# A fused transformer block on one core: constants, first stack and norm chain of the start-up arranged anew

## The chip, the cores and the metric

The kernel runs on one core of a Trainium2 chip. Its engines are TensorE (PE, with PEld for weight loads), VectorE (DVE), ScalarE (ACT), GpSimd (POOL) and SyncE (SP); DMAs are issued from SP and ACT. Each engine takes its instructions in the order of its own program and waits at semaphores. The metric is the time of one execution on the device, in microseconds, as the median of the runs. Lower is better.

## The reference

For eight batches of 512 tokens with 256 features: a modulated layer norm, causal attention with 16 heads of width 16, a gated residual; then a second modulated norm and a feed-forward block that itself starts with a norm (gain and bias), attention with 32 heads of width 8 without a mask, a residual, and an expert layer in which each half of a batch goes through one expert. All of it is f32.

```python
mod = (_silu(L0_c) @ L0_wmod).reshape(L0_c.shape[0], 6, 1, -1)
sa, ca, ga, sb, cb, gb = (mod[:, 0], mod[:, 1], ...)
h = _layernorm(x, axis=-1) * (1 + ca) + sa
x = x + ga * _L0_attn_ref(h, ...)          # causal, 16 heads of 16
h = _layernorm(x, axis=-1) * (1 + cb) + sb
x = x + gb * _L0_ffn_ref(h, ...)
...
xn = (x - mu) / jnp.sqrt(var + 1e-05) * ln_g + ln_b
att = jnp.einsum('bqhd,bkhd->bhqk', q, k) / np.float32(np.sqrt(hd))   # 32 heads of 8
o = jnp.einsum('bhqk,bkhd->bqhd', p, v).reshape(B, S, D) @ wo + x
h = jax.nn.gelu(jnp.einsum('metd,edf->metf', xe, w1) + b1[None, :, None, :], approximate=False)
y = jnp.einsum('metf,efd->metd', h, w2) + b2[None, :, None, :]
```

## The kernel before

**Plan.** One list of items, written out by hand in `sections()`, sets the order of the work; every engine walks the same list (`walk`) and takes from each item its own part. The sections are "start", "scale", "first", "second", "before" (together the start-up), "loop" (run six times) and "after". An item such as `("scores", 1, 0, 4, 2)` names kind, batch (0 or 1 ahead), attention (0 is the causal one, 1 the second), step and head of the step. `attention(main, lead, beside, ...)` lays out steps: for each position the scores of a step of `main`, the maxima of a step of `lead` (seven or eight steps ahead), the values of the step before, and from `beside` whatever is placed at a slot, four slots to a step. A step is a group of four heads and one 128-row tile; four steps make a group; the causal attention has 16 steps per batch, the second 32.

**Stacks.** Q and k are split into bf16 parts of which the matmuls need several (`qk`: ScalarE writes the top part at L937, VectorE the rest at L1399, GpSimd splits it at L794 and L796, SP stores the parts to DRAM at L711). `stacks` loads them as q_stack and k_stack, 8 heads to a unit (`load_stack`, L640). Three buffers of each are used in turn. The stacks also hold rows of constants: blank slices of q_parts (zeros) and eight rows of ones under each half of k_stack; they meet the rows of the maxima, which `max_rows` writes into q_stack (L730). Before, SP makes them by 12 DMAs from a tile of zeros and 6 from a tile of ones (L748 to L755), right after the first loads, behind two memsets of GpSimd (L781, L782).

**The start.** x of batch 0 is loaded and its norm begun ("start"); an inverse root is made by a first guess on VectorE (L1327 to L1331) and 13 Newton steps on GpSimd (L881 to L889). x of batch 1 is loaded into the same tile once batch 0 is normed. "first" has q and k of batch 0, with batch 1's statistics between the pieces; "second" has v and the first stack (q from SP, k from ACT). ACT issues all weight loads at its start, those of the feed-forward block too (L911), and VectorE rearranges two of them (L1510) before it enters "before".

**The second part of "before"** is the attention of batches 0 and 1, 32 steps in one row (`main`). It is laid out in two pieces, the first 24 steps and the last 8 (`half`). Beside steps 18 to 24 stand the first batch's output projection (L1241), its norm 1 with modulation (L1337, L1341) and the statistics of norm 2; between the pieces stand norm 2 (L1372), its turn to features, q and k of attention 2 (L1117) and their stack; the second piece has beside it v, and ahead of it the maxima of the first eight steps of attention 2 (L1413), two steps at a time in the first two positions.

## Time and profile before

| | |
|---|---|
| median of 3 runs | 1758.55 us (1752.73 to 1762.74) |
| profiled execution | 1755.25 us, span 1753.5 us |
| busy PE, DVE, ACT, POOL | 1495.6 (85%), 1153.1 (66%), 1007.8 (57%), 531.6 (30%) |
| chain that ended last | PE 64%, DVE 16%, ACT 8%, issue 5%, DMA 3% |
| granted TensorE clock, mean | 0.97 |

In the page's 40 slices, PE's digit is low in the first five (5, 6, 8, 6, 6), with PEclk below 9 in three of them; the DMA digit is 9 in the first. A timeline row gives start and length of an instruction or of several of one kind in a row, and in brackets how long its engine was idle before it and what ended that. A chain row gives one piece of the chain that ended last. A "q" behind an engine's name is its queue, that is, the issuing of DMAs.

### The profile page before, as it was taken

What the parts mean: (1) busy time and instruction counts of PE and PEld (TensorE: products, weight loads), DVE (VectorE), ACT (ScalarE), POOL (GpSimd) and SP (SyncE); (2) the same over time, 40 slices, a digit from 0 to 9 for tenths busy, and PEclk for the clock granted to TensorE, in tenths of its full rate; (3) what the DMA queues carried; (4) which work ended last, traced back from release to release, by engine and by line L of the source; (5) the groups of instructions that cost most, each with busy time, mean ns of one, the idle gap of its engine ahead of it and who ended that gap; (6) DMA issues with size and microseconds to landing.
All of it is one profiled execution on the core that took longest, in us unless ns stands there. A gap on an engine that the chain in (4) does not pass through costs nothing.

```text
span 1753.5 us, 30245 instructions
## 1 busy us (share of the span) xinstructions
PE 1495.6 (85%) x10001; PEld 662.1 (38%) x10001; DVE 1153.1 (66%) x2961; ACT 1007.8 (57%) x2096; POOL 531.6 (30%) x1245
## 2 busy tenths in 40 slices
PE   5686689988899889989899889998899887879767
PEld 4232323344333543345233443335333442314315
DVE  4566389755986469764996469763897458775430
ACT  1153357754677456754677456765577546666571
POOL 4233235222433134232343225231352224300100
PEclk9698799999999999999999999999999999999999
DMA  9550434423345233422443242342343232212201
GB/s 260 129 122 31 115 94 127 99 83 97 104 106 134 79 97 115 97 85 76 130 125 98 75 138 89 82 126 76 110 137 89 82 82 77 74 46 73 86 1 60
DMA packets 137542, 171.26 MB, mean 98 GB/s; under 512 B 17000, under 2 KB 103080, under 8 KB 137392
## 3 DMA queue, kind: packets, MB, share of 16 engines
q1 hardware_dynamic: 131568, 164.96, 33.8%
q10 hardware_dynamic: 5824, 4.37, 1.0%
q8 instruction: 86, 1.41, 0.3%
q14 instruction: 64, 0.52, 0.1%
HBM read 110.67 MB, written 56.66 MB: 95 GB/s over the span
## 4 chain that ended last, share of the span: by engine, by line
PE 64%; DVE 16%; ACT 8%; issue 5%; DMA 3%; POOL 2%; SPq 1%; ACTq 0%; POOLq 0%; DVEq 0%
PE bank_out L1198 16%; PE bank_scores L1179 10%; DVE neg_max L1413 8%; PE bank_max L1150 7%; PE bank_side L1285 7%; PE bank_side L1117 5%; ACT probs L976 5%; PE bank_side L1127 4%; PE bank_side L1269 3%; PE bank_scores L1269 3%; PE bank_side L1207 2%; PE bank_side L1241 2%; PE bank_side L1250 2%; DVE normed L1372 2%; DMA k_stack<-k_parts 1%
## 5 line engine op out<-in xcount | busy, mean ns | idle before, releaser
L976 ACT ACTIVATE probs<-bank_scores 128x512 f32<-128x512 f32 (+3 forms) x1536 | 753.2, 544 | 411.5 <-PE bank_scores L1179 394.2
L1413 DVE TENSOR_REDUCE neg_max<-bank_max 128x1 f32<-128x512 f32 x1024 | 653.1, 682 | 185.4 <-PE bank_max L1150 180.7
L1179 PE MATMUL bank_scores<-q_stack,k_stack 64*128 64x512 bf16 (+3 forms) x2048 | 318.0, 347 | 92.9 <-ACT probs L976 78.6
L1198 PE MATMUL bank_out<-probs,v_tile 128*9 128x512 f32 (+4 forms) x3072 | 368.7, 552 | 16.1 <-ACT out_raw L990 12.4
L1150 PE MATMUL bank_max<-k_stack,q_stack 64*128 64x512 bf16 (+3 forms) x2048 | 316.7, 345 | 73.6 <-DVE neg_max L1413 36.9
L1410 DVE CUSTOM_DVE_ANT_0 bank_max<-bank_max,causal 128x384 f32<-128x384 f32 (+3 forms) x512 | 241.8, 514 | 101.9 <-PE bank_max L1150 99.0
L1179 PEld LDWEIGHTS bank_scores<-q_stack,k_stack 64*128 64x128 bf16 x2048 | 84.9, 93 | 368.6 <-issue 348.0
L830 POOL TENSOR_SCALAR_AFFINE_SELECT probs<-probs 128x512 f32<-128x512 f32 x128 | 81.0, 633 | 351.3 <-ACT probs L976 351.2
L1150 PEld LDWEIGHTS bank_max<-k_stack,q_stack 64*128 64x128 bf16 x2048 | 105.6, 95 | 157.5 <-issue 108.6
L812 POOL CAST max_parts<-max_row 16x128 bf16<-16x128 f32 x96 | 28.4, 296 | 361.7 <-DVE max_row L1424 361.7
L1285 PE MATMUL bank_side<-w_out,hidden_T 128*128 128x256 f32 x512 | 118.8, 385 | 4.8 <-issue 2.7
L1285 PEld LDWEIGHTS bank_side<-w_out,hidden_T 128*128 128x128 f32 x512 | 94.6, 190 | 35.0 <-DVE max_row L1424 11.1
L1198 PEld LDWEIGHTS bank_out<-probs,v_tile 128*9 128x9 f32 (+1 forms) x3072 | 47.5, 91 | 133.7 <-issue 78.6
L1459 DVE TENSOR_TENSOR y_out<-bank_side,gb_bc 128x256 f32<-128x256 f32 x32 | 13.6, 425 | 122.9 <-PE bank_side L1285 122.9
L1117 PE MATMUL bank_side<-act_T,wk 128*128 128x256 f32 x236 | 67.4, 409 | 10.8 <-DVE rest L1399 6.5
L794 POOL CAST partsq<-rest 128x256 bf16<-128x256 f32 x64 | 25.4, 397 | 167.6 <-DVE rest L1399 167.6
L1117 PE MATMUL bank_side<-act_T,wq 128*128 128x256 f32 x232 | 69.0, 422 | 8.0 <-DVE act_T L1385 4.3
L1127 PE MATMUL bank_side<-wv,act_T 128*128 128x256 f32 x244 | 70.6, 413 | 4.3 <-ACT act_T L961 2.0
L1410 DVE DVE_READ_ACCUMULATOR2_ANT neg_max<- 128x1 f32 x512 | 72.3, 141 | 0.0
L1207 PEld LDWEIGHTS bank_side<-ident,out_raw 128*128 128x128 f32 x384 | 40.5, 141 | 74.8 <-issue 73.1
L1207 PE MATMUL bank_side<-ident,out_raw 128*128 128x128 f32 x384 | 62.6, 286 | 6.9 <-DVE rest L1399 3.5
L1269 PE MATMUL bank_side<-expert_xT,w_in 128*128 128x256 f32 x256 | 63.5, 391 | 1.5 <-DVE expert_xT L1452 0.9
(141 smaller groups left out, 1529.7 us busy)
## 6 DMA issues: line engine op xcount, KB each, us to landing
q_stack<-q_parts SPq DMA_DIRECT2D x128, 256.0 KB, 4.3
k_stack<-k_parts SPq DMA_DIRECT2D x122, 192.0 KB, 6.1
w_in<-in_L_ffn_w_dram SPq DMA_DIRECT2D x16, 1024.0 KB, 5.5
w_out<-in_L_ffn_w_dram SPq DMA_DIRECT2D x16, 1024.0 KB, 8.5
q_parts<-partsq SPq DMA_DIRECT2D x32, 384.0 KB, 2.6
k_parts<-partsk SPq DMA_DIRECT2D x32, 384.0 KB, 2.6
q_parts<-partsq SPq DMA_DIRECT2D x32, 256.0 KB, 2.9
k_parts<-partsk SPq DMA_DIRECT2D x32, 256.0 KB, 3.0
```

What stands on the lines that cost most here:

```text
L830: pool.affine_select(out=tile, in_=tile, compare_op=ALU.is_ge, fill=0.0, base=0, pattern=[[0, GROUP], [1, P]], channel_multiplier=-1).then ...
L976: nc.scalar.activation(probs[s % 2][:, head_at(k), q0:S], region[bank][:, q0:S], ACT.Exp, scale=float(WIDTH[a]) ** -0.5).then_inc(drained[ ...
L1117: ins = pe.matmul(region[bank][:, 0:S // 2], w_qkv[a][t][:, cc, oc * P:(oc + 1) * P], act_T[:, cc, cols], start=(cc == 0), stop=(cc == C - 1))
L1127: ins = pe.matmul(region[bank][:, 0:D], act_T[:, cc, t * P:(t + 1) * P], w_qkv[a][2][:, cc, :], start=(cc == 0), stop=(cc == C - 1))
L1150: ins = pe.matmul(region[to][:, 0:keys], q_stack[buf][rows, at, qt * P:(qt + 1) * P], k_stack[buf][rows, at, 0:keys], start=(i == 0), stop ...
L1179: ins = pe.matmul(region[to][:, q0:S], k_stack[buf][rows, at, kt * P:(kt + 1) * P], q_stack[buf][rows, at, q0:S], start=(i == 0), stop=last)
L1198: ins = pe.matmul(outb[32 * k:32 * k + WIDTH[a] + 1, q0:S], v_tile[a][:, kt, g * GROUP + k, :], probs[s % 2][:, k, q0:S], start=(kt == 0), ...
L1207: ins = pe.transpose(side[:, t * P:(t + 1) * P], out_raw[:, g % 2, t * P:(t + 1) * P], ident[:, :])
L1269: ins = pe.matmul(region[bank][:, k * EXP_TOK:(k + 1) * EXP_TOK], w_in[:, cc, ft * P:(ft + 1) * P], expert_xT[:, cc, j * EXP_TOK:(j + 1) * ...
L1285: ins = pe.matmul(region[bank][:, 0:D], hidden_T[:, ft, k * P:(k + 1) * P], w_out[:, ft, :], start=(ft == 0), stop=(ft == FT - 1))
L1410: v.tensor_tensor_reduce(region[bank][:, 0:keys], region[bank][:, 0:keys], causal[:, S - keys:S], 1.0, -3e38, ALU.add, ALU.max, dst).then_ ...
L1413: v.tensor_reduce(dst, region[bank], AX_X, ALU.max).then_inc(drained[bank], 1)
```

## The change

- The ones are no longer stored by DMAs: the whole of each k_stack is set to 1.0 on chip, two of the three by VectorE as its first work, the third (buffer 0) by GpSimd after its part of "first"; the loads write the product rows over it. GpSimd sets only a quarter of the zeros, and of the blank slices only those of batch 0's first attention are stored at the start (2 DMAs); the other 6 go out behind the first stack.
- The first stack is loaded by `load_first_stack` in two halves of four heads, 8 DMAs of half the size each for q and k; the first maxima wait for the first half (`half_loaded`), the fifth step for all.
- ACT issues the feed-forward weights after that stack; their rearranging on VectorE becomes the item `ffn_weights`, placed at slot 12 beside the first maxima. The expert bias has a semaphore of its own (`b1_in`).
- The Newton steps of norms 1 and 2 of batch 0 are taken by VectorE.
- The row of 32 steps is cut at step 20 instead of 24, norm 1 stands in one piece ahead of the eleventh maxima of batch 1, and the eight steps of attention 2's maxima stand one by one beside the last eight steps. Some loads (`stacks`, `load_mod`, `load_gate`) move by a slot or two.

```diff
@@ sections()
-    before = [("stacks", 0, 1)]
+    before = []
     beside = {}
+    place(beside, 4, [("stacks", 0, 1)])
+    place(beside, 12, [("ffn_weights", 0)])
...
-    place(beside, 25, [("stacks", 1, 0)])
+    place(beside, 22, [("stacks", 1, 0)])
...
-    place(beside, 79, norm_1[1:NEWTON_PIECE + 1], 0)
+    place(beside, 79, norm_1[1:], 0)
     place(beside, 82, [("load_residual", 1), ("load_gate", 0)])
-    place(beside, 83, norm_1[NEWTON_PIECE + 1:] + norm_2[:NEWTON_PIECE + 1], 0)
-    place(beside, 91, [("load_mod", 1)])
-    half = 3 * len(main) // 4
+    place(beside, 80, norm_2[:NEWTON_PIECE + 1], 0)
+    place(beside, 82, [("load_mod", 1)])
+    half = 20
     left = []
-    before += attention(main[:half], ahead[FIRST_LEAD:], beside, early, left, rows_after=(1, ROWS_AFTER),
+    before += attention(main[:half], ahead[FIRST_LEAD:half + FIRST_LEAD + 1], beside, early, left, rows_after=(1, ROWS_AFTER),
...
-    lead = [(), (), tuple(first_2[0:2]), tuple(first_2[2:4]), *one_each(first_2[4:])]
-    before += attention(main[half:], lead, beside, hand_on=handed)
+    lead = ahead[half + FIRST_LEAD + 1:]
+    lead += [()] * (len(main) - half - len(first_2) - len(lead)) + one_each(first_2)
+    before += attention(main[half:], lead, beside, hand_on=handed, rows_after=(1, ROWS_AFTER))
@@ load_first_stack, new
+        def load_first_stack(eng, dram, stack, rows):
+            per = GROUP // TILES
+            src = dram[0][0].rearrange("i (d h) s -> (i d) h s", d=WIDTH[0])[:, 0:UNIT_HEADS, :]
+            src = src.rearrange("(i r) (g t k) s -> g i t r k s", r=TILE_ROWS, t=TILES, k=per)
+            for g in range(UNIT_HEADS // GROUP):
+                for i in range(PASSES[0]):
+                    at = column_of(0, g, i, 0)
+                    for t in range(TILES):
...
+                        eng.dma_start(dst, src[g, i, t, 0:rows].rearrange("r k s -> r (k s)"))\
+                           .then_inc(stack_loaded[0] if g else half_loaded, 16)
@@ SyncE
-            sp.wait_ge(ones_made, 2)
-            for n in range(2):
...
-                        sp.dma_start(dst, blank[:, 0, :]).then_inc(ones_in, 16)
...
-                    sp.dma_start(k_stack[n][rows, :, :], ones.unsqueeze(1).broadcast_to([P // SLICES, UNIT_HEADS, S]))\
-                      .then_inc(ones_in, 16)
+            sp.wait_ge(blank_made, 1)
...
+            store_blanks(0, 0)
             walk(sp, {"load_x": load_x, "qk": qk, "stacks": stacks}, ("first", "second"))
+            for a, n in ((0, 1), (1, 0), (1, 1)):
+                store_blanks(a, n)
             sp.wait_ge(mod_rows_made, 4)
@@ GpSimd
-            pool.memset(ones, 1.0).then_inc(ones_made, 1)
-            pool.memset(blank, 0.0).then_inc(ones_made, 1)
+            pool.memset(blank[:, 0:2, :], 0.0).then_inc(blank_made, 1)
...
-                if piece == NEWTON_PIECE:
+                if piece == NEWTON_PIECE and not (b == 0 and n):
...
+            pool.memset(k_stack[0][:, :, :], 1.0).then_inc(ones_made, 1)
@@ ScalarE
-            for w, st in ((wq2, stage_w2[0]), (wk2, stage_w2[1]), (wv2, w_qkv[1][2][:, :, :]), (wo2, w_o[1][:, :, :])):
-                act.dma_start(st, w.rearrange("(c p) n -> p c n", p=P)).then_inc(ffn_weights_in, 16)
...
                 if u == 0:
+                    load_first_stack(act, k_dram, k_stack, products)
+                    for w, st in ((wq2, stage_w2[0]), (wk2, stage_w2[1]), (wv2, w_qkv[1][2][:, :, :]), (wo2, w_o[1][:, :, :])):
+                        act.dma_start(st, w.rearrange("(c p) n -> p c n", p=P)).then_inc(ffn_weights_in, 16)
@@ TensorE
+                if b == 0 and s == 0 and a == 0 and k == 0:
+                    pe.wait_ge(half_loaded, 16 * stack_dmas[0])
+                elif b == 0 and s == T_STEPS and a == 0 and k == 0:
+                    pe.wait_ge(stack_loaded[0], 16 * stack_dmas[0])
@@ VectorE
+                elif piece == NEWTON_PIECE:
+                    if b == 0 and n:
+                        for step in range(GUESS_STEPS, ROOT_STEPS):
+                            newton_step(dve, b, n, step)
...
+            for n in (buffer_of(0, 0), buffer_of(1, 0)):
+                v.memset(k_stack[n][:, :, :], 1.0).then_inc(ones_made, 1)
             walk(dve, {"layernorm": layernorm}, ("start",))
```

VectorE at its start, before (row number, line, operation, result<-input, partitions x elements):

```order
0 L1318 UNCONDITIONAL_BRANCH
1 L1354 BN_STATS stats<-x_in 128x6 x4
2 L1358 BN_AGGR mean_var<-stats 128x2 x4
3 L1327 TENSOR_SCALAR root<-mean_var 128x4
4 L1329 TENSOR_SCALAR root<-root 128x4
5 L1331 TENSOR_SCALAR rstd<-root 128x4
```

And now:

```order
0 L1348 UNCONDITIONAL_BRANCH
1 L1505 MEMSET k_stack 128x4096 x2
2 L1384 BN_STATS stats<-x_in 128x6 x4
3 L1388 BN_AGGR mean_var<-stats 128x2 x4
4 L1357 TENSOR_SCALAR root<-mean_var 128x4
5 L1359 TENSOR_SCALAR root<-root 128x4
6 L1361 TENSOR_SCALAR rstd<-root 128x4
```

The two memsets stand ahead of the statistics of the first x.

SP from its first loads on, before:

```order
2 L741 DMA w_in<-in_L_attn_q_proj_weight_dram 128x2x256
3 L741 DMA w_in<-in_L_attn_k_proj_weight_dram 128x2x256
4 L748 DMA q_parts<-x_res 128x512 x4
5 L751 DMA q_parts<-x_res 128x2x512 x2
6 L748 DMA q_parts<-x_res 128x512 x4
7 L751 DMA q_parts<-x_res 128x2x512 x2
8 L755 DMA k_stack<-y_out 16x8x512 x6
9 L656 DMA x_in<-in_L_attn_in_features_dram 128x4x256
10 L711 DMA q_parts<-partsq 128x3x512
```

And now:

```order
2 L782 DMA w_in<-in_L_attn_q_proj_weight_dram 128x2x256
3 L782 DMA w_in<-in_L_attn_k_proj_weight_dram 128x2x256
4 L792 DMA q_parts<-x_res 128x2x512 x2
5 L689 DMA x_in<-in_L_attn_in_features_dram 128x4x256
6 L744 DMA q_parts<-partsq 128x3x512
7 L744 DMA q_parts<-partsq 128x2x512
8 L744 DMA q_parts<-partsq 128x512
```

Sixteen DMAs are gone from between the first weights and the second x.

TensorE behind the last product of k of attention 2, where the second piece begins, before (bank_max are maxima, bank_scores scores, bank_out values; L1127 is v; the column count tells the step of a causal group: 512, 384, 256, 128 for scores and values, and the other way round for maxima):

```order
188 L1117 MATMUL bank_max<-act_T,wk 128x256 x2
189 L1179 MATMUL bank_scores<-q_stack,k_stack 128x512 x4
190 L1127 MATMUL bank_side<-wv,act_T 128x256 x2
191 L1179 MATMUL bank_scores<-q_stack,k_stack 128x512 x4
192 L1127 MATMUL bank_side<-wv,act_T 128x256 x2
193 L1179 MATMUL bank_scores<-q_stack,k_stack 128x384 x4
194 L1127 MATMUL bank_side<-wv,act_T 128x256 x2
195 L1179 MATMUL bank_scores<-q_stack,k_stack 128x384 x4
196 L1198 MATMUL bank_out<-probs,v_tile 17x512 x4
197 L1127 MATMUL bank_side<-wv,act_T 128x256 x2
198 L1179 MATMUL bank_scores<-q_stack,k_stack 128x256 x4
199 L1150 MATMUL bank_max<-k_stack,q_stack 128x512 x4
```

And now:

```order
166 L1143 MATMUL bank_max<-act_T,wk 128x256 x2
167 L1209 MATMUL bank_scores<-q_stack,k_stack 128x512 x4
168 L1180 MATMUL bank_max<-k_stack,q_stack 128x128 x4
169 L1153 MATMUL bank_side<-wv,act_T 128x256 x2
170 L1209 MATMUL bank_scores<-q_stack,k_stack 128x512 x4
171 L1180 MATMUL bank_max<-k_stack,q_stack 128x128 x4
172 L1153 MATMUL bank_side<-wv,act_T 128x256 x2
173 L1209 MATMUL bank_scores<-q_stack,k_stack 128x384 x4
174 L1180 MATMUL bank_max<-k_stack,q_stack 128x256 x4
175 L1153 MATMUL bank_side<-wv,act_T 128x256 x2
176 L1209 MATMUL bank_scores<-q_stack,k_stack 128x384 x4
177 L1180 MATMUL bank_max<-k_stack,q_stack 128x256 x4
```

Four steps of scores and causal maxima have moved from ahead of norm 2 to this place: scores, causal maxima (L1180) and v (L1153) in turn, where before there were scores and v alone, and the full maxima of attention 2 followed after two steps.

## Rows read from the trace of the kernel before

**Rows 1.** Stretches: us, busy PE, PEld, DVE, ACT, POOL, PEclk, DMA share, GB/s.
```profile
10.00:20.00 10.00, 9.10 (x36) 7.98 (x35) 5.35 (x14) 0.38 (x1) 1.77 (x8) 1.00 1.09 373
...
50.00:60.00 10.00, 5.62 (x32) 2.31 (x32) 6.61 (x27) 0.00 (x0) 0.00 (x0) 0.50 1.11 221
```

**Rows 2.** Chain of waits, first 60 us: start us, us, what.
```profile
16.41 12.55 DMA x_in<-_L_attn_in_features_dram
...
43.20 8.31 DMA k_stack<-k_parts
...
51.64 0.38 PE bank_max L1150 x3
```

**Rows 3.** Timeline, first 45 us: start, us, engine, work, [idle before <-releaser].
```profile
0.98 0.43 SPq L656 DMA_DIRECT2D x_in<-_L_attn_in_features_dram  x1
...
3.14 1.79 POOL L782 MEMSET x_res<- 128x2048 bf16 x1
...
5.56 1.40 DVE L1354 BATCH_NORM_STATS2 stats<-x_in 128x6 f32<-128x256 f32 x4 [5.56 <-DMA x_in<-_L_attn_in_features_dram]
...
7.28 0.17 DVE L1327 TENSOR_SCALAR root<-mean_var 128x4 f32<-128x4 f32 x1
...
7.48 0.17 DVE L1329 TENSOR_SCALAR root<-root 128x4 int32<-128x4 int32 x1
...
28.98 0.75 DVE L1354 BATCH_NORM_STATS2 stats<-x_in 128x6 f32<-128x256 f32 x2 [6.27 <-DMA x_in<-_L_attn_in_features_dram]
...
30.11 2.07 PE L1117 MATMUL bank_side<-act_T,wk 128*128 128x256 f32 x4 [5.70 <-DVE rest L1399]
...
33.87 0.67 POOL L796 TENSOR_TENSOR partsk<-rest,partsk 128x256 bf16<-128x256 f32 x1
...
39.80 2.61 SPq L640 DMA_DIRECT2D q_stack<-q_parts  x4
...
41.49 2.16 ACTq L640 DMA_DIRECT2D k_stack<-k_parts  x4
...
41.59 0.57 DVE L1510 COPY wq<-w_out 128x256 f32<-128x256 f32 x2
```

**Rows 4.** Timeline, the first maxima on VectorE.
```profile
52.16 0.30 DVE L1410 CUSTOM_DVE_ANT_0 bank_max<-bank_max,causal 128x128 f32<-128x128 f32 x1 [9.57 <-PE bank_max L1150]
...
61.92 0.70 DVE L1410 CUSTOM_DVE_ANT_0 bank_max<-bank_max,causal 128x512 f32<-128x512 f32 x1 [0.68 <-PE bank_max L1150]
```

**Rows 5.** Chain of waits, two values four steps apart, batch 1.
```profile
117.41 0.77 PE bank_out L1198 x8
...
128.17 0.77 PE bank_out L1198 x8
```

**Rows 6.** Timeline, from the first norm of batch 0 to the loop.
```profile
151.87 0.23 POOL L881 TENSOR_SCALAR root<-root 128x4 f32<-128x4 f32 x1 [1.39 <-DVE rstd L1331]
...
155.57 1.22 DVE L1337 SCALAR_TENSOR_TENSOR normed<-x,mean_var,mod_bc 128x256 f32<-128x256 f32 x2 [0.96 <-POOL rstd L889]
...
161.46 0.23 POOL L881 TENSOR_SCALAR root<-root 128x4 f32<-128x4 f32 x1 [5.34 <-DVE rstd L1331]
...
163.94 0.61 PE L1179 MATMUL bank_scores<-q_stack,k_stack 64*128 64x256 bf16 x4
...
168.20 0.28 PE L1179 MATMUL bank_scores<-q_stack,k_stack 64*128 64x128 bf16 x4
...
176.56 1.38 DVE L1372 TENSOR_SCALAR normed<-normed,mean_var,rstd 128x256 f32<-128x256 f32 x4
...
198.11 1.08 ACT L976 ACTIVATE probs<-bank_scores 128x512 f32<-128x512 f32 x2 [8.23 <-DMA k_parts<-partsk]
...
207.56 5.10 DVE L1413 TENSOR_REDUCE neg_max<-bank_max 128x1 f32<-128x512 f32 x8 [17.22 <-PE bank_max L1150]
...
219.47 1.04 PE L1179 MATMUL bank_scores<-q_stack,k_stack 64*128 64x512 bf16 x4
...
231.11 0.39 PE L1179 MATMUL bank_scores<-q_stack,k_stack 64*128 64x512 bf16 x2
```

91 lines of the change are left out of this document (50 added, 41 removed).

## The prediction, made before the changed kernel was run

> **What bounds the kernel now.** I read the busy time by stretches first, then the chain of waits, then the timeline where the chain waits. The first 236 of 1753.5 us are a start-up that is run once; after it come six equal turns of a loop and a tail, and the change leaves both word for word as they are. So only three places of the start-up count, and whatever is won there has to reach the first instruction of the loop, the scores at 231.11 [rows 6].
>
> Place A, up to the first attention matmul at 51.64 [rows 2]. Two transfers stand on the chain. The second batch's x is issued at 16.41, behind the 18 DMAs of constants on SP, and takes 12.55; VectorE stands idle 6.27 for it, with the splits of k queued behind, and TensorE 5.70 [rows 2, 3]. Then the last k_stack load, issued at 43.20, takes 8.31 [rows 2]. Place B, from there to about 149: the maxima, with a slow TensorE (granted clock 0.50 in 50 to 60, the 1.2 GHz level) and a full DMA share of 1.11 [rows 1]. Place C, from 149 to 231: the first batch's norms, then q and k of attention 2, their way through DRAM, and its first 32 maxima.
>
> All times below are times of the trace of before; "-8" means eight us earlier than there.
>
> **Place A.** Three edits act on it.
>
> (1) VectorE now begins with two memsets of a whole k_stack, 4096 bf16 elements each. The trace has no memset on VectorE. The nearest rows for its pace are its masked maxima, 0.30 us for 128 elements and 0.70 for 512: 1.04 ns per element [rows 4], so 4.3 for one and 8.5 for both. GpSimd's memset of 2048 in 1.79 [rows 3] would give 3.5 each at its pace. The engines begin within the first us (SP's first DMA is at 0.98 [rows 3]); VectorE would be free at 9.4, where its first statistics now start at 5.56 [rows 3]: **+3.8** for all that hangs on them. The other bound is nothing: if both memsets end within the 4.6 us up to 5.56 they are hidden under the load of x. I take 3.8, by VectorE's own row.
>
> The Trainium skill (VectorE: DVE Perf Modes, Zero memsets can be issued as uint32 (trn2)) says that a memset takes one cycle per element whatever its type; with the clock of its Specifications, 0.96 GHz, an estimate of 8.5 us for both, against this change. Its table of modes would give four elements per cycle to a bf16 operation within SBUF, 2.1 us for both, which the load hides. The trace shows neither; the sum would be 3.8 lower by the second.
>
> (2) The constants no longer stand ahead of x: two DMAs are left instead of 18, and the feed-forward weights (1 MB on ACT's queue) go behind the stack. x of batch 1 still waits for the normed tiles, so it is issued at about 17 as before, but finds empty queues; the first x took 4.6, from 0.98 to 5.56 [rows 3], so about 22, while VectorE wants it at 22.7 + 3.8 = 26.5. The wait of 6.27 goes. What is late next is the chain itself, 3.8 later: the rests of k come 6.27 - 3.8 = 2.5 earlier. GpSimd's splits then run back to back behind those of q: the eighth ends at about 32.5 instead of 34.54 [rows 3], -2.0, and the stores that followed to 39.80 [rows 3] land at 37.8. TensorE no longer has the gap of 5.70, and the product after it should take 1.0 and not 2.07 [rows 3]: its work up to the last v is -3.5, and ACT, which issued k_stack at 41.49 [rows 3] behind it, is free at 38.0. Issue of the stack: **-3.5** on ACT, -2.0 on SP.
>
> (3) The first maxima wait for half of a stack: four q and four k DMAs of half the size. Before, ACT's 768 KB took from 41.49 to 51.5, some 8 us of it flow, beside SP's 2.7 MB. Its half is 384 KB, so 4 us of flow after the same start of 1.5: 38.0 + 1.5 + 4.0 = 43.5. That is **-8.1** against 51.64, with all of (1) to (3). Bounds: -5 if the halves flow no better than the whole, -12 if the memsets are hidden as well. The second half is wanted a group of four steps of maxima later, and of the first group the last step is reached only at 61.92 [rows 4], 10 us after the start: hidden.
>
> **Place B.** The four copies of weights (L1510, two in 0.57 and two like them [rows 3]) leave a gap in which VectorE was idle and go between the first maxima, where VectorE sets the pace: **+1.0**. They wait for weights which ACT issues behind eight stack DMAs, at about 43 to 46. Late now are also six blank DMAs (1.5 MB) ahead of the second stack on SP. Some 6 MB then stand in the queues after 43.5. Saturated stretches moved 373 GB/s (10 to 20, when the blanks went) and 221 (50 to 60, the stacks) [rows 1]; so they end between 60 and 71. The copies come up at about 55 and could wait 0 to 3 us, with all maxima behind them; the first rows of maxima go to SP at about 60, behind the same queue, and are wanted at 69: between 9 us of slack and a wait of 2. The second stack is wanted at about 75. I take 0 for the waits and keep +4. Setting k_stack0 on GpSimd (about 3.5) ends long before GpSimd's next work, those first rows. The rest of B is a chain that shifts as it is.
>
> **Place C.** Four steps of the second attention (each: scores, values, four causal maxima) move behind q and k of attention 2, and 13 Newton steps of each of two norms move from GpSimd to VectorE.
> First norm: the Newton steps took 3.70, 151.87 to 155.57 [rows 6]; VectorE does a step of that size every 0.20 (7.28 to 7.48 [rows 3]), so 2.7: its last ends at 154.5. Then VectorE needs 5.9 for scaling, statistics and guess, as from 155.57 to 161.46 [rows 6]; two maxima (1.5), which used to lie under GpSimd's steps; 2.7 of Newton; two maxima (1.5); the turned rows and sums, 2.5. So the normed tiles of L1372 start at 168.6, not at 176.56 [rows 6]: **-7.9**, though four steps were done in those 7.9.
> The chain from there to ACT's restart at 198.11 [rows 6] is unchanged: 190.2.
> From the restart to the tenth step of the second attention before took 207 - 198.1 = 8.9, for nearly two steps and three v products; the same with two steps' maxima (1.4 us of TensorE): 10.3, so 200.5. Two more steps at the steady pace of a causal step, (128.17 - 117.41)/4 = 2.69 [rows 5], and two transposes with their copies, 1.5: 207.4. Then eight steps with one step of attention 2's maxima each: four of these took 231.11 - 219.47 = 11.64 [rows 6], so 23.3: the loop starts at 230.7. **-0.4.** What the earlier norm gives, the moved steps take back; VectorE's 32 full maxima, from 207.56 to about 231 before [rows 6], start no sooner. Bounds: -4, if the steps fit into its pauses better; +6, if the four steps run at the 4.25 us of the step at 163.94 to 168.19 [rows 6].
>
> **The sum.** -8.1 + 1.0 - 0.4 = **-7.5**. The profiled execution took 1755.25 (span 1753.5), so 1747.8 for one like it. The three timed runs have a median of 1758.55 and lie between 1752.73 and 1762.74; the four together have a mean of 1757.3. I put the median after at **1750**, between what each base gives.
>
> **Rivals.**
> R1, the memsets are hidden: VectorE writes bf16 faster than its f32 rows. -3.8 more, so -11.3: 1746. It holds if one memset takes under 2.3. For: nothing else is on VectorE there; against: every row of VectorE in this trace is near 1.04 ns per element.
> R2, the transfers that are sent late collide: the weight copies wait 3, the first rows of maxima 1 to 2, in the DMA-bound stretch of share 1.11 [rows 1]. -3: 1754.
> R3, the four moved steps run at the pace of 4.25 instead of 2.69: +6, so -1.5: 1756. For: TensorE comes out of the 8.23 that ACT waits [rows 6] in front of them. Against: the 11.64 for four steps behind it.
> R4, slower. SP must load the second stack of attention 2 only after the values of step 8, which now come after it in the order, and the rows of maxima for step 12 are queued behind that wait on SP. If all 12 steps of C run at 4.25 in this way, they take 51 instead of 34: +17, so +9.5: 1767. It decides from a pace of 3.5 on; the steady rows [rows 5] speak against it.
> R5, the change does not do what it says: x of batch 1 lands late all the same. It still waits for the norm, but with 2 MB less ahead a landing later than 26.5 would need twice the 4.6 of the first. -3: 1754.
>
> **Chances.** Forecast 0.50, R1 0.18, R2 0.10, R3 0.12, R4 0.05, R5 0.05. About 0.5% (8.8 us) is what a measurement of this kernel can tell from no change, and the forecast lies just within it; with an error of some 4 us on it, 0.5 x 0.45 of it is beyond, with R1 nearly all, and a little of the rest: faster 0.44, same 0.51, slower 0.05. Range: R1 less its spread of the runs, 1741, to R3 with the same, 1759.
>
> **What would show it.** Right: two VectorE memsets of about 4.3 each before 9.4; no DMA wait of x before the rests of k; first maxima near 43.5; the four weight copies without a wait; L1372's tiles of the second norm some 8 us sooner against the first maxima's shift; the loop's first scores near 223.6; equal turns of the loop. Wrong: memsets of 1 us; first maxima later than 46; a wait of VectorE for weights; a distance from the first maxima to the loop's first scores that differs from 180 by more than 3.

## The result, and the profile after

The changed kernel takes a median of 1748.2 us (8 runs, 1745.76 to 1751.3); the kernel before took 1757.53 beside it (8 runs, 1752.73 to 1762.74). The ratio is 0.9946, with a 95% interval of 0.9929 to 0.9962: 9.3 us less, where the forecast had 8.5 less and 1750. That is 0.54%, just beyond the 0.5% that the forecast took for what can be told from no change, and the interval leaves out 1. The profiled execution is the slowest of the eight: 1751.3, span 1749.4. The one of the kernel before, 1755.25, was quicker than its median, so the two traces end only 4.1 us apart where the medians are 9.3 apart.

Place A in the timeline of the changed kernel (start, us, engine, line, work, count, [idle before <- releaser]); it answers to [rows 3]:

```profile
1.71 3.47 DVE L1505 MEMSET k_stack<- 128x4096 bf16 x1 [1.71 <-PEq L1568]
5.98 3.47 DVE L1505 MEMSET k_stack<- 128x4096 bf16 x1 [0.80 <-issue]
9.37 1.34 DVE L1384 BATCH_NORM_STATS2 stats<-x_in 128x6 f32<-128x256 f32 x4
27.26 0.74 DVE L1384 BATCH_NORM_STATS2 stats<-x_in 128x6 f32<-128x256 f32 x2
36.49 3.51 POOL L916 MEMSET k_stack<- 128x4096 bf16 x1
36.79 3.49 DVE L1544 TENSOR_SCALAR hidden_T<-hidden_T 8x512 f32<-8x512 f32 x1
45.62 0.40 PE L1180 MATMUL bank_max<-k_stack,q_stack 64*128 64x128 bf16 x4 [7.25 <-DMA k_stack<-k_parts]
```

The memsets end in time for statistics at 9.37 (before: 5.56). The statistics of batch 1 at 27.26 have no idle time in front of them: the wait of 6.27 for x is gone. The first maxima start at 45.62, 6.0 earlier than in [rows 2]. The chain of waits of the changed kernel (start, us, what) shows how they came in: three issues of ACT, then the fourth with its landing.

```profile
38.47 0.36 ACTq L656
38.86 0.53 ACTq L656
39.42 0.60 ACTq L656
40.05 5.44 DMA k_stack<-k_parts
45.62 0.38 PE bank_max L1180 x3
```

Two more landmarks cut the rest: the first product of the first attention's output (its first matmul on wo, 142.49 before) and the loop's first scores (231.11 before, 223.01 after). Stretches between them (us, busy time of PE, PEld, DVE, ACT, POOL, granted clock, DMA share, GB/s), the kernel before first:

```profile
51.64:142.49 90.85, 74.50 (x591) 29.99 (x591) 58.84 (x236) 37.77 (x95) 27.89 (x58) 0.84 0.41 99
142.49:231.11 88.62, 58.56 (x387) 27.14 (x385) 49.08 (x136) 29.66 (x73) 29.27 (x72) 0.81 0.27 75
```

and the changed kernel:

```profile
45.62:137.65 92.03, 75.37 (x591) 30.40 (x591) 59.67 (x240) 37.76 (x95) 27.88 (x58) 0.83 0.57 141
137.65:223.01 85.36, 54.86 (x387) 27.07 (x384) 52.84 (x162) 29.42 (x73) 24.05 (x46) 0.82 0.28 79
```

So in this pair of traces: 6.0 won up to the first maxima, 1.2 lost in place B, 3.3 won in place C, 8.1 in all at the loop's start. Behind it the changed kernel took 1526.4 to its end and the kernel before 1522.4. A granted clock of 0.50 is the lower level, 1.2 GHz; a clock of c over a stretch of length L means 2(1 - c)L at that level. That is 31.3 us of place B after and 29.1 before (the clock is given to 0.01, so such a figure is good to about 1 us). This second quantity, which the edits don't set directly, goes with much of what the landmarks leave over.

### The profile page after: what moved, and what is told of

Read it like the earlier page. It is cut to its first block, busy times and chain, and to the rows that moved or that the text cites. A ratio compares the mean times of both kernels' runs of the same rounds, so it can differ in the third digit from the quotient of the medians.

```text
span 1749.4 us, 30247 instructions
## 1 busy us (share of the span) xinstructions
PE 1495.2 (85%) x10001; PEld 662.9 (38%) x10001; DVE 1166.8 (67%) x2989; ACT 1007.4 (58%) x2096; POOL 528.3 (30%) x1219
## 4 chain that ended last, share of the span: by engine, by line
PE 65%; DVE 17%; ACT 8%; issue 5%; DMA 2%; POOL 1%; SPq 1%; ACTq 0%; POOLq 0%; DVEq 0%
PE bank_out L1228 16%; PE bank_scores L1209 10%; DVE neg_max L1456 8%; PE bank_max L1180 7%; PE bank_side L1315 7%; PE bank_side L1143 6%; ACT probs L1002 5%; PE bank_side L1299 4%; PE bank_side L1153 3%; PE bank_scores L1299 3%; PE bank_side L1237 2%; PE bank_side L1271 2%; PE bank_side L1280 2%; DVE normed L1406 2%; PE bank_side L1118 1%
## 5 line engine op out<-in xcount | busy, mean ns | idle before, releaser
L1180 PE MATMUL bank_max<-k_stack,q_stack 64*128 64x512 bf16 (+3 forms) x2048 | 316.2, 344 | 70.1 <-DVE neg_max L1456 35.9
L1180 PEld LDWEIGHTS bank_max<-k_stack,q_stack 64*128 64x128 bf16 x2048 | 105.6, 95 | 154.8 <-issue 107.5
L1153 PE MATMUL bank_side<-wv,act_T 128*128 128x256 f32 x244 | 69.8, 409 | 4.3 <-ACT act_T L987 2.0
L1016 ACT ACTIVATE out_raw<-bank_out 128x512 f32<-128x512 f32 x96 | 58.2, 606 | 12.0 <-PE bank_out L1228 12.0
```

The lines of the kernel that those rows point to most:

```text
L1153: ins = pe.matmul(region[bank][:, 0:D], act_T[:, cc, t * P:(t + 1) * P], w_qkv[a][2][:, cc, :], start=(cc == 0), stop=(cc == C - 1))
L1180: ins = pe.matmul(region[to][:, 0:keys], q_stack[buf][rows, at, qt * P:(qt + 1) * P], k_stack[buf][rows, at, 0:keys], start=(i == 0), stop ...
```

## The experiments

All are compared with the kernel before by ratio, beside which they ran. The table is for all of them; the times are landmarks of one profiled execution each, "slow" is the time at the lower level worked out as above, with the stretch's own granted clock. The last column is the time from the loop's first scores to the end of the span.

```
kernel            ratio [95%]             median   first   to product   to loop       loop    behind
                                                  maxima   us   (slow)   us   (slow)
before            -                       1757.5   51.64  90.85 (29.1)  88.62 (33.7)  231.11  1522.4
changed           0.9946 [0.9929,0.9962]  1748.2   45.62  92.03 (31.3)  85.36 (30.7)  223.01  1526.4
e1_half_memset    0.9915 [0.9901,0.9929]  1742.6   42.81  88.13 (21.2)  85.47 (30.8)  216.41  1523.5
e2_hold_second    0.9941 [0.9927,0.9956]  1747.5   43.88  93.40 (33.6)  85.73 (30.9)  223.01  1524.7
e3_split24        0.9979 [0.9964,0.9993]  1754.2   46.25  90.75 (29.0)  91.99 (40.5)  228.99  1529.8
e4_prologue_only  0.9966 [0.9951,0.9980]  1752.3   45.18  92.33 (33.2)  87.24 (27.9)  224.75  1526.0
e5_newton_pool    0.9936 [0.9919,0.9953]  1747.8   45.29  89.22 (25.0)  84.54 (30.4)  219.05  1522.0
e6_whole          0.9967 [0.9954,0.9981]  1752.0   49.14  91.21 (31.0)  84.98 (30.6)  225.33  1522.4
e7_weights_early  0.9942 [0.9922,0.9962]  1748.5   45.39  91.04 (29.1)  86.62 (34.6)  223.05  1524.8
e8_all            0.9933 [0.9913,0.9952]  1745.4   40.55  93.00 (33.5)  86.05 (31.0)  219.60  1523.0
e9_warm           0.9907 [0.9888,0.9927]  1742.6   45.96  88.64 (26.6)  86.08 (34.4)  220.68  1522.2
e10_best          0.9902 [0.9883,0.9922]  1739.2   42.30  90.33 (27.1)  83.19 (26.6)  215.82  1520.0
e11_half_pool     0.9917 [0.9901,0.9934]  1743.3   41.53  90.67 (29.0)  84.72 (30.5)  216.92  1526.8
e12_split_alone   0.9988 [0.9974,1.0002]  1755.9   51.98  90.80 (30.9)  84.83 (30.5)  227.61  1527.2
```

### The memsets: e1_half_memset

```
-                v.memset(k_stack[n][:, :, :], 1.0)
+                v.memset(k_stack[n][:, :, :].rearrange("p h s -> p (h s)").bitcast(F32), 1.0019378662109375)
```

> The changed kernel with one edit: each of VectorE's two memsets writes its stack as 2048 f32 elements whose bits are two bf16 ones, instead of 4096 bf16 elements. Same bytes, half the elements. The trace of the changed kernel has 3.47 us for each, and the first statistics at 9.37. Theory (a memset is paid per element, and all of it lies on the path to the first maxima): 1.74 each, statistics at 5.9, which is after the landing of x at about 5.5; x of batch 1 is issued 3.4 earlier and still lands before it is wanted; first maxima at 42.2 instead of 45.62, the loop's first scores at 219.6 instead of 223.01, median 3.4 below the changed kernel's: 1745. Rival (paid per byte): 3.47 each again, nothing moves, 1748. Rival (the memsets are only partly on the path, because x of batch 1 or TensorE's own chain is next): 1.74 each, but the first maxima only 1 to 2 earlier, with a DMA named as VectorE's releaser before the statistics of batch 1.

Timeline of e1_half_memset:

```profile
1.28 1.76 DVE L1508 MEMSET k_stack<- 128x2048 f32 x1 [1.28 <-PEq L1571]
3.42 1.76 DVE L1508 MEMSET k_stack<- 128x2048 f32 x1 [0.38 <-issue]
5.73 1.41 DVE L1387 BATCH_NORM_STATS2 stats<-x_in 128x6 f32<-128x256 f32 x4 [0.55 <-DMA x_in<-_L_attn_in_features_dram]
42.81 0.40 PE L1183 MATMUL bank_max<-k_stack,q_stack 64*128 64x128 bf16 x4 [7.46 <-DMA q_stack<-q_parts]
```

Read these rows by their ends. In the changed kernel the two memsets end at 5.18 and 9.45, 4.27 apart; here at 3.04 and 5.18, 2.14 apart. The starts of such rows are not to be trusted: the first has nothing of this program ahead of it that differs, yet it is given as 1.71 for 4096 elements and as 1.28 for 2048, and the idle time between the two shrinks with them, from 0.80 to 0.38. Taken back from the ends, VectorE begins at 0.91 in both. So the memset is paid by the element, 1.04 ns for each: 4.27 for 4096, 2.14 for 2048 of twice the size. Both now end 0.55 before x lands, and of the 3.64 won at the statistics 2.81 reach the first maxima. So most of the 3.8 of the forecast lay on the path. The second rival of the expectation holds in part: what the chain of waits of e1_half_memset now begins with is not the memset but the load of k's weights, which TensorE waits for until 9.21, and which the memsets had covered in the changed kernel:

```profile
2.01 7.06 DMA w_in<-_attn_k_proj_weight_dram
9.21 1.94 PE bank_max L1092 x8
```

The median gained more than that and more than the theory's 3.4: 5.6 against the changed kernel, with intervals that only touch, at 0.9929. The mean granted clocks of the timed runs (0.976 in its four, 0.974 in the changed kernel's eight) make that an estimated 6 us less at the lower level. The traces have 6.6 less at the loop: 2.8 up to the first maxima, and 3.9 between the first maxima and the first product, where the slow clock ended at 60, while in the changed kernel it lasted until about 74. The first two rows are e1_half_memset's (56 to 64), the others the changed kernel's:

```profile
56.00:60.00 4.00, 3.63 (x17) 1.72 (x17) 2.06 (x12) 0.38 (x1) 1.39 (x4) 0.50 1.08 197
60.00:64.00 4.00, 2.01 (x14) 0.95 (x13) 3.16 (x13) 0.39 (x2) 1.59 (x4) 1.00 1.06 254
```

```profile
60.00:64.00 4.00, 3.12 (x16) 1.50 (x15) 2.03 (x11) 0.38 (x1) 1.99 (x6) 0.50 1.09 183
72.00:76.00 4.00, 3.66 (x20) 1.51 (x16) 2.63 (x8) 2.36 (x5) 1.59 (x4) 0.80 0.00 0
```

### The half stack: e2_hold_second and e6_whole

e2_hold_second:

```
             for g in range(UNIT_HEADS // GROUP):
+                if g:
+                    eng.wait_ge(half_loaded, 16 * stack_dmas[0])
```

> The changed kernel with one edit: SP and ACT issue the second half of the first stack only when all eight DMAs of the first half have landed. My forecast had the first half in at 43.5; it came at 45.48, with the second half's DMAs issued from 40.1 on into the same queues, at 226 GB/s in 40 to 44. Theory (the second half takes bandwidth from the first): 896 KB of first halves at that 226 GB/s take 4.0, from 38.1 plus 1.5: first maxima at 43.6, -2.0; the second half is issued at 44 and wanted some 13 us after the first maxima, so it isn't waited for; weights of the second attention land 3 to 4 later, and VectorE's copies of them, at 57.2, wait 0 to 2. Loop's first scores at 221 to 223, median 1746 to 1748. Rival (the halves have a latency of their own, not shared bandwidth): first maxima at 45.6 as before and all else later or equal: 1748 to 1751.

The chain of waits of e2_hold_second:

```profile
37.37 0.54 SPq L658
37.95 0.59 SPq L658
38.58 0.60 SPq L658
39.22 4.53 DMA q_stack<-q_parts
```

The first maxima came at 43.88, 1.74 earlier; but the issue began 0.75 earlier too (37.37 for 38.12 on SP). From SP's first issue to the first maxima it is 6.5 us here, 6.7 in e8_all, which holds back too, and 7.0 to 8.2 in the nine kernels, the changed one among them, that don't and wait for a half only. Counted from ACT's first issue, which ended the wait in the changed kernel, it is 6.5 for 7.2. Holding back is worth 0.7 to 1.0, up to half of what the theory gave it, and the landing itself still takes 4.53. At the loop nothing is left: 93.40 to the product with 33.6 slow, for 92.03 with 31.3. The medians, 1747.5 and 1748.2, can't be told apart.

e6_whole:

```
                     pe.wait_ge(half_loaded, 16 * stack_dmas[0])
+                    pe.wait_ge(stack_loaded[0], 16 * stack_dmas[0])
```

> The changed kernel with one edit: TensorE waits for both halves of the first stack before the first maxima (the sixteen DMAs are issued as they are). Measures what the halves are worth. In the changed kernel the last DMA of k's second half is issued at 43.2 and takes some 5.5. Theory (what is won at the first maxima comes out at the end, less what the slow clock takes of it): first maxima at 48.5 to 49.5, 3 to 4 later; by the line through ten traces (first maxima to first attention_out product: 88.1 us where 20.6 of it are at the slow clock, 93.4 where 33.5 are) the loop's first scores 2 to 4 later, 225 to 227, median 1750 to 1752. Rival (the slow stretch ends where it ends, so the halves are worth half of that): 224.5, median 1750. Second rival (nothing of it reaches the loop, as with the second half held back, whose 1.74 was gone there): 223, 1748.

First maxima at 49.14, 3.5 later than in the changed kernel, the loop's 2.3 later, the median 3.8 higher with intervals that overlap a little (from 0.9954, up to 0.9962). By these figures the halves are worth 2 to 4 of the 9.3; the medians alone don't show it clear of noise. Chain of waits of e6_whole: SP issues eight DMAs one after the other, then this:

```profile
42.35 6.65 DMA q_stack<-q_parts
49.14 0.38 PE bank_max L1181 x3
```

### The order of the transfers: e7_weights_early

```
+            for w, st in ((wq2, stage_w2[0]), (wk2, stage_w2[1]), (wv2, w_qkv[1][2][:, :, :]), (wo2, w_o[1][:, :, :])):
+                act.dma_start(st, w.rearrange("(c p) n -> p c n", p=P)).then_inc(ffn_weights_in, 16)
 (at ACT's start; taken out behind load_first_stack)
```

> The changed kernel with the four DMAs of the second attention's weights (1 MB) back at ACT's start, ahead of all else that matters, as before the change; constants still set on chip. Tells whether x of batch 1 was late because of the 18 constants on SP or because of what stood in the queues altogether. Theory (SP's own constants were what held it): x of batch 1 is issued at 16.9 and lands by 23, no DMA wait of VectorE before the statistics at about 27, first maxima at 45.6; the four weights are out of place B's way: equal, 1748. Rival (the queues are shared, any megabyte ahead delays it): a wait of VectorE of 1 to 4 for x of batch 1, first maxima at 46.5 to 49, median 1749 to 1752.

Nothing moved: statistics of batch 1 at 26.34 without a wait, first maxima at 45.39, median 1748.5. So it was the constants on SP that held x, and not the weights by themselves; sending the weights late is worth nothing by itself. (Constants on SP without the weights were not run.)

### Place C: e3_split24, e5_newton_pool, e4_prologue_only, e12_split_alone

e3_split24 has the split and places of the kernel before, Newton steps on VectorE:

```
-    half = 20
+    half = 3 * len(main) // 4
-    lead = ahead[half + FIRST_LEAD + 1:]
-    lead += [()] * (len(main) - half - len(first_2) - len(lead)) + one_each(first_2)
+    lead = [(), (), tuple(first_2[0:2]), tuple(first_2[2:4]), *one_each(first_2[4:])]
...
```

> The changed kernel with the second attention's split put back to step 24 and the norms' places, the load of mod and the second stack's place of the kernel before; the Newton steps of the two norms stay on VectorE. The two traces give the stretch from the first maxima to the loop's first scores as 179.5 before and 177.4 after, 3.3 of it won behind step 80.  Theory by my forecast (the split gives as much as it takes; what was won is the Newton steps, 3.70 - 2.6 = 1.1 for each norm, and pauses): loop's first scores at 223 to 224, median 1748 to 1749. Rival (the split is worth something by itself, since the moved steps fill pauses of TensorE beside the scores of attention 2): loop's first scores at 225 or later, median 1750 to 1751. Second rival (the split costs): 221 to 222, 1746.

e5_newton_pool has the split at 20 and the Newton steps on GpSimd:

```
-                if piece == NEWTON_PIECE and not (b == 0 and n):
+                if piece == NEWTON_PIECE:
 (and VectorE's branch for it empty)
```

> The changed kernel with the 13 Newton steps of the two norms of batch 0 back on GpSimd, the split left at step 20. The steps take 3.70 there (0.29 each) and 2.6 on VectorE (0.20 each), but on VectorE nothing else goes beside them: TensorE stands idle for 7.95 from 145.7 on. Theory by my forecast (each move gives 1.1 less nothing): loop's first scores 2 later, at 225, median 1750. Rival (the two pairs of maxima, 1.5 each, that VectorE can do under GpSimd's steps make up for the slower steps): loop's first scores at 222 to 223.5, median 1747 to 1749.

e4_prologue_only undoes both, by the two diffs above together:

> The changed kernel with both edits behind the first attention undone: split at step 24 as before, and the Newton steps of the two norms on GpSimd. What is left is the prologue: memsets, order of transfers, half stack, weight copies. By the landmarks of the two traces at the end of the first attention (values at 112.56 for 117.41, 137.72 for 142.56) the prologue's gain is 4.84 and nothing behind it changes: loop's first scores at 226.3, median 4.8 below the kernel before, 1752.7 where that has 1757.5. By my forecast, in which the edits behind it gave 0.4: loop's first scores at 223.4, 1748.6. If the prologue's gain is lost behind it (transfers that come up earlier than their data): over 228.

e12_split_alone is the kernel before with e3_split24's diff the other way round:

```
-    half = 3 * len(main) // 4
+    half = 20
...
```

> The kernel before with the second attention's split at step 20 and the norms' places that go with it; prologue and Newton steps as before. My forecast for this part (with the Newton steps) was 0.4. The traces with the new prologue say: split with Newton steps on GpSimd 84.5 us from the first attention_out product to the loop's first scores (30.7 of it at the slow clock), no split 87.2 (27.3 at the slow clock); the kernel before 88.6 (34.2 slow). Theory (the split alone is worth 3 to 4): 84.5 to 86 us there, loop's first scores at 227 to 228.5, median 3.5 below the kernel before, 1753.5 to 1754.5. Rival (it is worth that only together with the Newton steps or the prologue): loop at 230 to 231, median within 1 of the kernel before.

The four and the two kernels of the start make a table of place C, from the first product to the scaled tiles of the second norm (the start of its L1372 or L1406) and to the loop:

```
                        Newton on GpSimd            Newton on VectorE
split at step 24        34.1, 88.62 (before)        37.5, 91.99 (e3)
                        34.5, 87.24 (e4)
split at step 20        23.8, 84.54 (e5)            25.2, 85.36 (changed)
                        23.8, 84.83 (e12)
```

e4_prologue_only has the prologue alone: 0.9966, some 6 us less than the kernel before (5.2 by its median), so all that stands in place C is worth the other 3 to 4. Its median of 1752.3 is near the 1752.7 that the landmarks gave it, its loop at 224.75 sooner than their 226.3. e3_split24's theory, that the split gives as much as it takes, fell: the loop at 228.99 for 223 to 224, the median 1754.2 for 1748 to 1749.

The split is what brings the tiles 10 to 12 us sooner. At the loop 2.7 (e4 to e5), 3.8 (before to e12) and 6.6 (e3 to the changed kernel) of that are left; the last pair has 9.8 us less at the lower level, so its figure is the clock's in part. In the medians it is 5.3 us (0.9966 to 0.9936, intervals that overlap by a hair), 5.8 (0.9979 to 0.9946, intervals that don't overlap), and 1.6 on the old prologue, where the interval runs from 4.6 won to 0.4 lost. The rival that the split is worth something by itself holds with the new prologue. On the old one e12_split_alone reached the loop at 227.61, inside its theory's 227 to 228.5, but its median of 1755.9 lies between the theory's and the rival's. So the size isn't settled: 2.7 and 3.8 in the two pairs of traces whose clocks are nearest.

The Newton steps on VectorE cost. With the split at 20 it is 1.4 more until the tiles and 0.8 more to the loop, at about the same time at the slow clock (30.4 and 30.7); with the split at 24 it is 3.0 more until the tiles (e4 to e3), and 4.7 to the loop with 12.6 more slow. Each step is quicker on VectorE (starts 0.20 apart, before 0.29). At the first norm this helps a little: TensorE's wait ahead of the next maxima is 7.95, and 9.13 with the steps on GpSimd. At the second norm it costs more than that. On GpSimd the steps run beside a pair of maxima of VectorE, on VectorE ahead of it, and TensorE waits 5.03 for it instead of 2.42. Timelines of the changed kernel, then of e5_newton_pool:

```profile
147.17 0.16 DVE L666 TENSOR_TENSOR root<-rstd 128x4 f32<-128x4 f32 x1
153.63 1.04 PE L1180 MATMUL bank_max<-k_stack,q_stack 64*128 64x512 bf16 x4 [7.95 <-DVE neg_max L1453]
160.25 0.38 PE L1189 MATMUL bank_side<-ident,neg_max 128*16 128x128 f32 x1 [5.03 <-DVE neg_max L1453]
```

```profile
151.66 1.04 PE L1180 MATMUL bank_max<-k_stack,q_stack 64*128 64x512 bf16 x4 [9.13 <-DVE neg_max L1451]
155.68 0.38 PE L1189 MATMUL bank_side<-ident,neg_max 128*16 128x128 f32 x1 [2.42 <-DVE neg_max L1451]
```

The medians agree in sign (1747.8 for 1748.2; 1752.3 for 1754.2) and can't tell it from nothing.

### The clock: e9_warm, e8_all

e9_warm:

```
             walk(pe, {"v": v}, ("second",), in_pieces=True)
+            for k in range(80):
+                pe.matmul(outb[:, k % 4 * P:(k % 4 + 1) * P], zeros[:, :], zeros[:, :], start=True, stop=True)
             pe.wait_ge(pro_drained, 9)
```

> The changed kernel with 80 extra matmuls of zeros (128x128 bf16, start and stop set, into the still unused bank that is zeroed there anyway) between TensorE's last v and the first maxima, where it is idle from 38.4 to 45.6. They compute nothing that is used. In the changed kernel TensorE's granted clock is 0.50 from 44 to 74, in the kernel before from 44 to 78, with half as many f32 elements per memset from 40 to 60; from the first maxima to the first product of attention_out these take 92.0, 91 and 88.1. Theory (the clock is a cause: the 1.2 us lost between the first maxima and the end of the first attention, and the 3.9 won there by the halved memsets, are the time at the slow clock, not the weight copies): with TensorE busy before, the granted clock is 1.00 at the first maxima or falls later, the slow stretch ends sooner, and the loop's first scores come 3 to 8 earlier, at 215 to 220; median 1740 to 1745. Rival (VectorE's maxima and copies set the pace and the clock follows): granted clock changes or not, the loop's first scores at 222 to 224. Second rival (the extra matmuls last longer than the wait): first maxima later than 45.6 by what they overrun, and all behind them.

Timeline of e9_warm, then its stretches at the first maxima and over place B:

```profile
37.76 4.63 PE L1341 MATMUL bank_out<-zeros 128*128 128x128 bf16 x80
45.96 0.40 PE L1180 MATMUL bank_max<-k_stack,q_stack 64*128 64x128 bf16 x4 [3.57 <-DMA q_stack<-q_parts]
```

```profile
44.00:48.00 4.00, 0.79 (x8) 0.29 (x8) 1.52 (x9) 0.00 (x0) 0.00 (x0) 0.68 1.07 212
45.96:134.60 88.64, 73.27 (x590) 29.75 (x590) 59.61 (x240) 37.78 (x95) 27.99 (x58) 0.85 0.57 145
```

Work that nobody uses made the kernel 5.6 us quicker, 0.9907 against 0.9946, with intervals that don't overlap. In the profiled execution the first maxima came 0.3 later and the product 3.05 earlier: place B took 88.64 instead of 92.03, with 26.6 at the lower level instead of 31.3. The clock fell later (0.68 over 44 to 48, where the changed kernel has 0.50), and not never. The loop came at 220.68, just outside the 215 to 220 of the theory; the median lies inside its range.

One trace alone wouldn't carry this, for e5_newton_pool, whose program is the changed kernel's up to the product, took 89.22 over place B without any zeros. The timed runs carry it. Each has a mean granted clock of its own: 0.973 to 0.977 in the eight of the changed kernel, with a mean of 0.974, and 0.976 to 0.981 in the six of e9_warm, with a mean of 0.978. Over the span that is an estimated 13 us less at the lower level, and at 0.4 us for each (the slope over the traces, given under place B in the next section), 5 to 6 us: all that was gained. So the clock is a cause here and not only a sign. In the profiled execution 2.3 of the gain lie before the loop and 4.2 behind it; why a warm start-up should shorten the end as well stays open, and one trace is no proof that it does so each time.

e8_all has the diffs of e1_half_memset and e2_hold_second, and GpSimd's memset as f32 too:

```
-            pool.memset(k_stack[0][:, :, :], 1.0)
+            pool.memset(k_stack[0][:, :, :].rearrange("p h s -> p (h s)").bitcast(F32), 1.0019378662109375)
```

> The changed kernel with three edits together: VectorE's two memsets and GpSimd's one as 2048 f32 elements with the bits of two bf16 ones, and the second half of the first stack issued only when the first has landed. Alone, the first gave first maxima at 42.81 and the loop's first scores at 216.4; the holding back gave first maxima 1.74 earlier and nothing at the loop. What GpSimd's memset tells: in the changed kernel VectorE's scaling of the gates, 8x512 f32, stands for 3.49 beside GpSimd's memset of 3.51 (36.49 to 40.00), where such an operation took 0.4 before. Theory (VectorE's operation is held up while GpSimd's memset runs): memset 1.8, and the scaling 1.8 as well. Rival (it is something of the operation itself, its first touch of hidden_T): 3.49 stays. Times: if the first maxima decide, 41.1 and the loop at 215, median 1741; if the stretch at the granted clock 0.50 decides (it ended at 74 with and without the holding back), as with the memsets alone: 216.4, median 1742.6.

It has the earliest first maxima of all, 40.55, and neither theory's time: 93.00 to the product with 33.5 slow, loop at 219.60, 3 later than the rival had it. The memset took 1.80, but the scaling of the gates came ahead of it and so tells nothing here. Its runs spread from 1743.05 to 1752.02, around a median of 1745.4. Against e1_half_memset it started place B 2.3 sooner and reached the product 2.6 later.

### Together: e10_best and e11_half_pool

e11_half_pool has the three memsets as f32 and e5_newton_pool's diff; e10_best has them too, and e9_warm's loop:

```
-            for k in range(80):
+            for k in range(110):
```

> A version that might beat both kernels: the changed kernel with the three memsets as 2048 f32 elements, the Newton steps of the norms on GpSimd, and 110 matmuls of zeros between the last v and the first maxima. Alone, the halved memsets had a median of 1742.6, the zeros 1742.6, the Newton steps on GpSimd 1747.8, for 1748.2 of the changed kernel. Theory (zeros and earlier start act on the same slow stretch, and add up in part): first maxima at 42.8, 88 us to the first attention_out product, then 84.5 to the loop: 215.5, median 1739 to 1741. Rival (the slow stretch takes it back, as in the kernel with held second half and halved memsets, 93.0 us from the first maxima on): loop at 219 to 220, median 1744 to 1746.

> The kernel of e10_best without the zeros: the three memsets as 2048 f32 elements and the Newton steps of the norms on GpSimd. Against e10_best it tells what the zeros do to the clock once more. Theory (earlier first maxima are worth their 2.8, the rest of the 5.6 that the halved memsets gave was a slow stretch that ended 12 us sooner and needn't do so here): first maxima at 42.8, loop at 216 to 220, median 1743 to 1745. Rival (the halved memsets are worth 5.6 always): loop at 215.5 and median 1742. Also: VectorE's scaling of the gates takes 0.41 if it comes before GpSimd's memset, 1.8 to 2.0 if it comes beside it.

e10_best is the quickest: 1739.2, 0.9902 of the kernel before (0.9883 to 0.9922), 1% less, and below the changed kernel with intervals that don't overlap. Its theory held: the loop at 215.82 for 215.5, the median inside 1739 to 1741. Between the two, 0.9902 and 0.9917, the intervals overlap, so what the zeros add on top isn't shown. Nor does this pair of traces put it where e9_warm's did: the zeros let TensorE stand only 1.39 ahead of the first maxima, but the clock fell to 0.50 at about 46 all the same, and the product came at 132.63 with them and at 132.20 without. What e10_best is ahead lies behind that, 1.5 in place C and 6.8 behind the loop's start. The halved memsets gave 4.9 here together with the Newton steps (0.9917 for 0.9946, intervals that overlap by a hair), first maxima at 41.53 and the loop at 216.92, within the theory's 216 to 220; the rival's 1742 isn't excluded either. The scaling of the gates is taken up in the last section.

## Why the prediction was right, point by point

The time, the sign and the range held. The sum of -7.5 came out as -8.1 at the loop, but two of its terms were off, place A by 2.1 too much and place C by 2.9 too little, and that they made up for each other is luck. The forecast's own measure shows it: from the first maxima to the loop it had 180 and allowed 3, and 177.4 were measured.

**Memsets, +3.8: right, and by the right parts.** VectorE was free at 9.45 and began the statistics at 9.37, for the forecast 9.4. The rows give 3.47 for each memset, but their ends give 4.27 and a start of 0.91, as worked out under e1_half_memset: the 4.3 and the first us of the forecast. So the row that was nearest was indeed VectorE's own maxima, 1.04 ns per element. R1, memsets hidden under the load of x, would have needed less than 2.3 for one, and fell. e1_half_memset built that case with 2.14, and it is worth 5.6 in the median, where R1 put 3.8. The Trainium skill (VectorE: DVE Perf Modes, Zero memsets can be issued as uint32 (trn2)) says that a memset goes by elements and not by bytes, one to a cycle; with the clock of its Specifications that is an estimate of 4.27 for one. The trace agrees in both, with 4.27 between the ends and 2.14 for half the elements; a pattern that isn't zero, packed the same way, took the same.

**x of batch 1: right.** No wait, statistics at 27.26 for the forecast 26.5; R5 fell. The parts were stored, and SP issued the stack, at 38.12 for 37.8, ACT at 38.47 for 38.0.

**The half stack: the one step of place A that failed.** The forecast took it as 1.5 to start and 4.0 of flow, 5.5 in all. It was three issues, 0.36 to 0.60 each, then a fourth that had landed 5.44 after its start: 7.0. The step that failed is that flow of 4.0. With the second half held back the last DMA still took 4.53; so of the 1.5 that were missing 0.7 to 1.0 are the second half's share of the queues. The rest isn't taken apart, nor is it shown what of the 4.53 is latency and what the flow of the first halves. First maxima at 45.62, not 43.5: -6.0, not -8.1; in the other traces with the same prologue 45.2 to 46.3.

**Place B, +1.0: the amount right, its cause wrong.** The copies (L1415) ran at 57.16 without a wait, and behind the first maxima no engine is shown to wait in place B for a weight or a row of maxima; R2 fell. But kernels with the copies and with the kernel before's 29 us at the slow clock take as long as it: e3_split24 90.75 (29.0 slow), e7_weights_early 91.04 (29.1), before 90.85 (29.1) without them. They cost nothing that can be seen. What the changed kernel lost, 1.2, goes with 2.2 more at the slow clock. Over the fourteen traces a straight line gives 0.41 us per us at the lower level for this stretch (correlation 0.94): 0.9 of the 1.2. It is a correlation, and e5_newton_pool (89.22, 25.0 slow) shows that the same program can lose or win 2.8 here from one execution to another.

**Place C, -0.4: the step that was mis-sized most.** It came out as -3.3. The forecast of tiles 7.9 sooner was near, 8.9; that was credited in part to the Newton steps, which in fact cost 1.4 of it, and 0.8 at the loop. The working of what the moved steps take back failed: +7.5 between ACT's restart and the loop (40.5 for 33.0), where 37.43 were measured, +4.4. The 10.3 for the first two steps and three v products were made from a stretch with v products of 2.07 and 1.94 at the slow clock. TensorE in the kernel before and, below, in the changed one:

```profile
199.82 2.07 PE L1127 MATMUL bank_side<-wv,act_T 128*128 128x256 f32 x4
202.58 1.94 PE L1127 MATMUL bank_side<-wv,act_T 128*128 128x256 f32 x4
205.86 1.13 PE L1127 MATMUL bank_side<-wv,act_T 128*128 128x256 f32 x4
```

```profile
187.50 2.07 PE L1153 MATMUL bank_side<-wv,act_T 128*128 128x256 f32 x4
190.22 1.13 PE L1153 MATMUL bank_side<-wv,act_T 128*128 128x256 f32 x4
192.92 1.13 PE L1153 MATMUL bank_side<-wv,act_T 128*128 128x256 f32 x4
```

TensorE was back at the full clock one product sooner, and the stretch took 8.40 instead of 10.3. That is luck for the most part, and not what the maxima between the products do: e7_weights_early and e9_warm have the same order of work there, their second product took 2.06 and 1.95 (e7_weights_early's below), and their stretch 9.80 and 9.68.

```profile
189.33 2.06 PE L1153 MATMUL bank_side<-wv,act_T 128*128 128x256 f32 x4
```

The next two steps took 6.06 for 6.9, and the last eight 22.97 for 23.3. R3 and R4, a pace of 4.25, fell: at most 38.8 from ACT's restart to the loop in any kernel with this split, for the forecast 40.5. Lost again were 1.2 between the tiles and ACT's restart (22.7 for 21.6), where TensorE's q and k of attention 2 were longer at the slow clock.

**Behind the loop's start: forecast as unchanged, and it isn't quite.** The turns are equal, but the time from the loop's first scores to the end differs by up to 9.8 us among the fourteen traces (1520.0 to 1529.8). Summed over pieces of 10 us, the time at the lower level there lies between 17.6 (e10_best) and 37.6 (e3_split24, e12_split_alone), three quarters of it or more in the last 320 us, and a straight line gives 0.40 us for each (correlation 0.95). The changed kernel's profiled execution has 30.6 and the kernel before's 27.2, 1.4 of the 4.0 that it gave back. The medians, over several executions, have gained 9.3: the forecast took what is behind the loop's start as unchanged, and one pair of traces can't test that to better than these 4 us.

## What to carry to other kernels

Where the clock falls in a wait and stays low behind it, a start that is earlier by some us is worth anything from nothing (e2_hold_second, 1.7) to over twice that (e1_half_memset, 2.8 for 6.6) at the loop of one trace: compare the time at the lower level in both traces before crediting an edit, and price a stretch with rows of the clock that the new neighbour will leave there. A load cut in halves is in when the last of its issues has landed, so count the issues and one full landing (here 1.6 to 1.9 and 4.5 to 5.4), not bytes over bandwidth. Time a memset by the ends of its rows. A short serial chain isn't quicker on the faster engine if that engine had work to do beside it.
